# Building the owner matrix of overflow rows: a comparison, a product with ones and a second comparison in place of a comparison and a multiplication

## The reference, cut to what matters

```python
# layer 0
h = jnp.maximum(_layernorm(x, axis=-1), 0.0)
mask = (adj > 0.0).astype(x.dtype)
xj_proj = x @ W1a                                  # here x is h, 64 -> 192
diff = x[:, :, None, :] - x[:, None, :, :]
h = jax.nn.relu(xj_proj[:, :, None, :] + diff @ W1b + b1)
hm = jnp.einsum('bjkh,bjk->bjh', h, mask)          # sum over the neighbours k of node j
deg = jnp.sum(mask, axis=-1)
x = x + hm @ W2 + deg[..., None] * b2
# layer 1
h = jnp.maximum(_layernorm(x, axis=-1), 0.0)
x = x + einsum('bnf,of->bno', einsum('bnm,bmf->bnf', adj, h), W)
```

## Time and profile before

| | |
|---|---|
| median of 3 runs | 916.15 us (915.91 to 916.58) |
| profiled execution, its own time | 916.14 us |
| its span, first to last instruction | 914.0 us |
| around the span | 2.1 us |
| granted TensorE clock, mean | 0.985 |
| VectorE (DVE) busy | 882.5 us, 97% |
| TensorE (PE) busy | 861.5 us, 94% |
| ScalarE (ACT) busy | 775.9 us, 85% |
| GpSimd (POOL) busy | 693.2 us, 76% |
| DVE's share of the chain that ended last | 79% |

### The profile page before, as it was taken

One profiled execution on the slowest core, in us unless ns is written; L12 is line 12 of the kernel. 1 busy time (PEld: TensorE's weight loads), 2 busy tenths in 40 slices (PEclk: granted clock), 3 DMA queues, 4 the chain that ended last, 5 costly groups with the idle time before them and its releaser, 6 DMA issues.

```text
span 914.0 us, 28230 instructions
## 1 busy us (share of the span) xinstructions
PE 861.5 (94%) x8626; PEld 772.5 (85%) x8627; DVE 882.5 (97%) x3544; ACT 775.9 (85%) x1728; POOL 693.2 (76%) x1548
## 2 busy tenths in 40 slices
PE   3869999999999999999999999999999999999996
PEld 1448898889888989898889888888988898889895
DVE  6989999999999999999999999999999999999993
ACT  4858889888888888888888888988888888888883
POOL 0857787878787878787877878787878787878774
PEclk9799999999999999999999999999999999999997
DMA  8500000000000000000000000000000000000000
GB/s 338 240 1 2 8 3 8 8 7 9 8 7 8 2 8 8 8 7 8 7 3 8 8 8 8 8 8 7 3 8 7 8 8 8 8 8 2 7 8 16
DMA packets 8120, 19.21 MB, mean 21 GB/s; under 512 B 1312, under 2 KB 5920, under 8 KB 6944
## 3 DMA queue, kind: packets, MB, share of 16 engines
q1 hardware_dynamic: 7056, 16.98, 4.9%
q10 hardware_dynamic: 912, 0.39, 0.2%
HBM read 13.17 MB, written 4.19 MB: 19 GB/s over the span
## 4 chain that ended last, share of the span: by engine, by line
DVE 79%; issue 15%; POOL 2%; PE 2%; DMA 1%; ACT 1%; SPq 0%; ACTq 0%; POOLq 0%
DVE acc L740 43%; DVE onehot_space L726 16%; DVE onehot_row L783 4%; DVE owner L777 3%; DVE stats L801 3%; DVE PQ L657 3%; DVE x_all L792 2%; DVE mv L769 2%; DVE x_all L795 2%; POOL rstd L894 1%; DMA x_all<-x_nbf_dram 1%; PE ring L336 1%; PE ring L327 0%; ACT mask_all L501 0%; ACT code_jk L503 0%
## 5 line engine op out<-in xcount | busy, mean ns | idle before, releaser
L740 DVE SCALAR_TENSOR_TENSOR acc<-ring,acc 128x384 f32<-128x384 f32 x896 | 488.3, 545 | 4.8
L507 ACT COPY ring<-P 128x768 f32<-128x768 f32 x512 | 403.4, 811 | 25.2 <-DVE acc L740 20.5
L357 PE MATMUL ring<-PQ,onehot_space 128*128 128x192 f16 x4096 | 402.3, 246 | 22.0 <-ACT ring L507 19.1
L357 PEld LDWEIGHTS ring<-PQ,onehot_space 128*128 128x128 f16 x4096 | 338.0, 99 | 43.7 <-DVE onehot_space L726 27.6
L843 POOL TENSOR_TENSOR relu_row<-relu_row 128x192 f32<-128x192 f32 x256 | 154.8, 605 | 117.5 <-ACT relu_row L539 107.4
L726 DVE TENSOR_SCALAR onehot_space<-mask_all 128x256 f16<-128x256 f16 x1024 | 226.6, 237 | 0.0
L560 ACT ACTIVATE h<-x_all,shift,rstd 128x64 f32<-128x64 f32 x128 | 56.2, 439 | 87.1 <-POOL shift L862 87.1
L830 POOL TENSOR_SCALAR start<-P,spare 128x192 f32<-128x192 f32 x128 | 120.4, 941 | 6.1 <-ACT P L553 5.0
L443 PE MATMUL post<-consts,acc 128*128 128x128 f32 x512 | 98.5, 274 | 1.5 <-POOL relu_row L843 1.5
L444 PE MATMUL post<-ownerT,relu_row 128*128 128x128 f32 x512 | 99.0, 275 | 0.0
L385 PE MATMUL ring<-PQ,owner 128*128 128x384 f16 (+1 forms) x512 | 94.5, 307 | 0.0
(11 more groups left out here) (129 smaller groups left out, 1590.1 us busy)
## 6 DMA issues: line engine op xcount, KB each, us to landing
adj_all<-adj_kbj_dram SPq DMA_DIRECT2D x8, 1024.0 KB, 17.9
x_all<-x_nbf_dram SPq DMA_DIRECT2D x8, 512.0 KB, 18.5
out_dram<-x_all SPq DMA_DIRECT2D x32, 128.0 KB, 1.7
consts<-consts_dram SPq DMA_DIRECT2D x1, 192.0 KB, 2.6
onehot_space<-w1a_dram ACTq DMA_DIRECT2D x2, 48.0 KB, 4.4
onehot_space<-w1b_dram ACTq DMA_DIRECT2D x2, 48.0 KB, 6.7
onehot_space<-b_dram ACTq DMA_DIRECT2D x1, 96.0 KB, 10.0
w2a<-w_dram ACTq DMA_DIRECT2D x1, 32.0 KB, 11.1
```

What stands on the lines that cost most here:

```text
L357: last = nc.tensor.matmul(to, hot(s), parts[:, part, H:2 * H], start=False, stop=(part == 1), skip_group_check=True)
L507: return nc.scalar.copy(slots[to], src.unsqueeze(1).unsqueeze(1).broadcast_to([N, BANKS, PER_BANK, H]))
L740: return nc.vector.scalar_tensor_tensor(sums, slots[to][:, bank_], 0.0, start[:, :, :] if first else sums, ALU.max, ALU.subtract if first ...
```

## The change

The owner matrix gets another formula. `reached` is one at (j, r) if r is below `end_row[j]`. `end_row` grows with j, so the number of ones in a column r is the number of nodes whose rows end after r; a product of a 128x128 matrix of ones with `reached` gives this number on every partition. If node j owns r, the nodes j to 127 are those, and their number is `left[j]` = 128 - j, a constant per partition. So `owner` is the comparison of these numbers with `left`. `from_first` and the two instructions L774 and L777 go.

In their place VectorE runs, in step b at i = 2 and behind the three L783, one comparison for `owner` of graph b+1 and one for `reached` of graph b+2. TensorE multiplies the ones with `reached` in step b at i = 0, ahead of the transpose L402, into 128 columns of the bank `post` beside the row codes. ScalarE's copy L544 takes 256 columns in place of 128. Graph 0 gets its product and copy by themselves ahead of the loop, and `left` is summed once while the inputs load.

```diff
-        from_first = sb("from_first", [N, N], F16)
+        reached = sb("reached", [N, N], F16)
+        left = sb("left", [N, 1])
...
-        code_row = sb("code_row", [N, N], F16)
+        row_codes = sb("row_codes", [N, 2, N], F16)
+        code_row, owner_code = row_codes[:, 0, :], row_codes[:, 1, :]
...
 # TensorE, step, i == 0
+                        if exists(b + 1):
+                            pe.wait_ge(reached_ready, b + 2)
+                            nc.tensor.matmul(owner_code_ps, ones_h[:, :], reached[:, :], start=True, stop=True)
                         nc.tensor.matmul(ownerT_ps, own, ident_h[:, :], start=True, stop=True).then_inc(rows_summed, 1)
...
 # TensorE, ahead of graphs
+            pe.wait_ge(reached_ready, 1)
+            nc.tensor.matmul(owner_code_ps, ones_h[:, :], reached[:, :], start=True, stop=True).then_inc(first_summed, 1)
...
 # ScalarE, step, i == 1
-                        nc.scalar.copy(code_row[:, :], code_row_ps)
+                        parts = slice(0, 2 if exists(b + 1) else 1)
+                        nc.scalar.copy(row_codes[:, parts, :], row_codes_ps[:, parts, :])
...
 # ScalarE, ahead of graphs
+            act.wait_ge(first_summed, 1)
+            nc.scalar.copy(owner_code, owner_code_ps).then_inc(first_owner_ready, 1)
...
 # VectorE
-            nc.vector.tensor_tensor(upto, before, ident, ALU.add)
+            chain(nc.vector.tensor_tensor(upto, before, ident, ALU.add))
+            nc.vector.tensor_reduce(left[:, :], upto, AX_X, ALU.add).then_inc(left_ready, 1)
...
+            def owners(b, u):
+                nc.vector.tensor_scalar(owner[:, u % 2, :], owner_code, left[:, 0:1], None, ALU.is_equal).then_inc(owner_ready, 1)
+            def reach(b):
+                nc.vector.tensor_scalar(reached[:, :], count_h[:, :], end_row[:, bass.ds(b, 1)], None, ALU.is_lt).then_inc(reached_ready, 1)
...
-                    if i == 0 and exists(b + 1):
-
-                        if main:
-                            dve.wait_ge(owner_ready, b + 1)
-                        nc.vector.tensor_scalar(from_first[:, :], count_h[:, :], first_row[:, at], None, ALU.is_ge).then_inc(from_ready, 1)
-                    if i == 1 and exists(b + 1):
-                        dve.wait_ge(from_ready, b + 2)
-                        nc.vector.scalar_tensor_tensor(owner[:, (u + 1) % 2, :], count_h[:, :], end_row[:, at], from_first[:, :], ALU.is_lt,
-                                                       ALU.mult).then_inc(owner_ready, 1)
                     if i == 2 and main:
...
                         last.then_inc(onehot_row_ready, 1)
+                        if exists(b + 1):
+                            owners(b + 1, u + 1)
+                        if exists(b + 2):
+                            reach(b + 2)
...
+            reach(0)
             lead(step)
+            dve.wait_ge(left_ready, 1)
+            dve.wait_ge(first_owner_ready, 1)
+            owners(0, 0)
+            reach(1)
             graphs(nc.vector, step, load_any(nc.vector))
```

More of the change, by code:

```diff
@@ L168, in gnn_kernel @@
         h1T_ps = post[:, 3 * N:4 * N]
-        code_row_ps, ownerT_ps = post[:, 0:N], post[:, N:2 * N]
+        row_codes_ps, ownerT_ps = post[:, 0:2 * N].rearrange("p (k n) -> p k n", k=2), post[:, 2 * N:3 * N]
+        code_row_ps, owner_code_ps = row_codes_ps[:, 0, :], row_codes_ps[:, 1, :]
         consts_in = sem("consts_in")
@@ L207, in gnn_kernel @@
         onehot_ready = sem("onehot_ready")
-        from_ready = sem("from_ready")
+        left_ready = sem("left_ready")
+        reached_ready = sem("reached_ready")
+        first_summed = sem("first_summed")
+        first_owner_ready = sem("first_owner_ready")
         owner_ready = sem("owner_ready")
@@ L744, in step @@
                 main = exists(b)
-                at = bass.ds(b + 1, 1)
                 for i in range(CHUNKS):
@@ L782, in step @@
                         for s in range(ROW_SLOTS):
-                            last = nc.vector.tensor_scalar(onehot_row[:, s, :], code_row[:, :], 2.0 * (COVERED + s) + 1.0, None,
+                            last = nc.vector.tensor_scalar(onehot_row[:, s, :], code_row, 2.0 * (COVERED + s) + 1.0, None,
                                                            ALU.is_equal)
                         last.then_inc(onehot_row_ready, 1)
+                        if exists(b + 1):
+                            owners(b + 1, u + 1)
+                        if exists(b + 2):
+                            reach(b + 2)
                     if i == 3 and exists(b - 2):
```

## The result

The changed kernel takes 920.94 us (median of 5 runs, 920.63 to 921.50) against 916.05 (915.81 to 916.58): 1.0053 of the time before, 95% interval 1.0039 to 1.0068. It is slower by 4.9 us.

The account below looks back on a forecast made before the run. VectorE was taken to set the pace, held in places by GpSimd. Per graph +0.19 (leaving L830 later), -0.19 (L830 earlier) and -0.01 gave -1.3 us: 916.14 to 914.8, taken as 915; own range 911 to 921, with rivals 897 to 929.

Parts of the forecast that it names:

- L830 holds the group, and VectorE leaves it at a fixed distance behind L830's start, whatever was saved before: Chunk 2: GpSimd's L830 holds VectorE's three L783 in its first 0.29 or so; they end 0.66 behind its start.
- L830 comes 0.19 earlier: GpSimd's chain: shorter L859, L843 and L862 bring L830 earlier by 0.15 in long graphs, 0.23 in short, 0.19 mean.
- Rival 3: GpSimd's L859 keeps its 700 ns, L830 stays, VectorE leaves later: 936, half the shift 926; chance 0.22 with its halves.
- `owners` and `reach` cost 0.135 each: VectorE, chunk 2: each new comparison costs what an unheld L774 does, 0.135, with bounds 0.10 and 0.33.
- VectorE goes on to L657 0.93 behind L830 in place of 0.74, 0.19 later: VectorE after chunk 2's group: 0.66 for the held three plus 0.27 for the new two, slower by 0.19 a graph.
- +0.19 - 0.19 - 0.01: Sum per graph: VectorE leaves L830 later, L830 comes earlier, an L726 in chunk 3 no longer meets GpSimd; -1.3 us in all.
- The next L726 is held in L774's stead in long graphs: VectorE behind the aggregate: L726 0.23 behind L843 lasts 0.41, so the long graph gains 0.14 there, not 0.33.
- TensorE and ScalarE hide their parts: TensorE's extra matmul, 0.06, fits a 0.19 gap; ScalarE's wider copy, 0.13, is hidden by its wait for L862.
- the forecast's sign: ScalarE's wait for GpSimd's L862 falls by about 0.13, and by as much again as L859 gets shorter.
- TensorE's gathers: What would make the forecast wrong at the root: VectorE waiting for gathers, with about 0.4 less lead over chunk 2's consumes.
- Rivals 1 and 2: First: VectorE not held, GpSimd's L830 gives way, 901, chance 0.2. Second: nothing held, ScalarE and GpSimd limit, 895.5, chance 0.13.
- The plain sum of VectorE's time: VectorE: 0.50 removed, two comparisons added, nothing held differently: 0.22 less a graph, 28 us for 127 graphs.

Follow-up runs that it names:

- the run with constants: Changed kernel with a constant in place of the value per partition in both new comparisons, so the owner matrix is not right: 909.01 us, ratio 0.9922.
- the old places: New formula with `reached` behind the aggregate of chunk 0 and `owner` behind the consumes of chunk 1: 903.44 us, ratio 0.9862 to the kernel before.

## Why the prediction was wrong, step by step

The forecast was 915, hardly a change, with faster (0.47) more likely than slower (0.33). Measured was 920.9, 4.9 slower and clear of no change. The mechanism was found and one term was mis-sized. That 920.9 lies at the edge of the forecast's own 911 to 921 is luck: 921 stood for L830 coming only 0.14 earlier, and it came 0.20 earlier. (The range's other end, a shift of 0.23, gives 910 by the forecast's own sum, not 911.)

- *L830 holds the group, and VectorE leaves it at a fixed distance behind L830's start, whatever was saved before.* Right: in the steady graphs L852 starts about 0.22 ahead of the group, and both the run with the group in chunk 1 and the one with the subtraction first move the time as this says.
- *L830 comes 0.19 earlier.* Right: 4.29 behind L809 in both kinds, 0.16 and 0.24 earlier, 0.20 in the mean; the power L859 fell to 572 ns. Rival 3, which decides below 0.19, is out.
- *`owners` and `reach` cost 0.135 each.* Wrong, this is the step that failed. They cost 0.163 each, 0.056 more in a graph, 7 us. The price was taken from L774 behind the aggregate. The trace of before had it elsewhere too, at 55.11 and 60.21, where its distance to the next start is 0.16:

```profile
60.21 0.24 DVE L774 TENSOR_SCALAR from_first<-count_h,first_row 128x128 f16<-128x128 f16 x1
60.37 0.22 DVE L726 TENSOR_SCALAR onehot_space<-mask_all 128x256 f16<-128x256 f16 x1
```

- *VectorE goes on to L657 0.93 behind L830 in place of 0.74, 0.19 later.* Both are ends, 0.08 longer than the starts; in starts the forecast is 0.85 in place of 0.66. Measured is 0.92 in place of 0.66, 0.26 later. Of the 0.07 too few, 0.056 are the price above, the rest is the three one-hot comparisons (0.59 behind L852's start, not 0.58).
- The sum with what was measured is +0.26 - 0.20 - 0.03 = +0.03 a graph, 4 us; the forecast had +0.19 - 0.19 - 0.01. The -0.03 is the L726 of chunk 3 that no longer meets GpSimd: 0.18 in long graphs before (412.10 to 412.28), 0.13 now. That accounts for the 4.4 us of the graphs.
- *The next L726 is held in L774's stead in long graphs.* Right, but it lasts 0.33 (at 410.75) and not 0.41. It starts 0.34 behind L865 and not 0.23, since the two L741 ahead of the statistics now take 0.39 (409.10 to 409.49) in place of 0.29 before (406.38 to 406.67). The forecast missed that, and a hold of 0.07 on the L741 of chunk 1 (at the second L865). The first is taken up by the hold behind it at L865, as the run with constants shows; for the second the hold by L852 should do the same, but no run takes it away by itself.
- *TensorE and ScalarE hide their parts.* Right, shown by the run with them alone. The copy grew by 0.106, forecast 0.13. ScalarE's wait for GpSimd's L862 fell by 0.28 a graph (87.1 to 51.2 us), as the forecast's sign had it. VectorE does wait for TensorE's gathers, but for 1.7 us in all, in four places (0.2 before).
- Rivals 1 and 2 are out: something is held in every steady graph.

The plain sum of VectorE's time, 28 us less, would have been far off; the old places give 12.5 us.

## What to carry to other kernels

Where VectorE sets the pace and GpSimd runs beside it, an instruction's place relative to GpSimd's is part of its price: the same two comparisons made the kernel 12.5 us faster or 5 us slower. Lay the start times of both engines over one period before moving anything, and price an instruction by the distance to the next start in more than one neighbourhood. A saving ahead of a hold is worth nothing; one behind it counts until the next hold.

## What the runs showed of the hardware

- GpSimd's L852 (one input of 192 columns, 0.94 long in the profile) held a fast 16-bit VectorE instruction until 0.28 to 0.29 after its own start (406.60 here, 404.56 with the subtraction first). The subtraction L891 (two inputs, 0.55) held one until 0.36 (`reached` issued twice) or 0.42 (the subtraction first) after its start, and the first L865 (two inputs, 0.59) until between 0.40 (`reached` ahead of the aggregate) and 0.49 (410.41 here). The Trainium skill (SBUF — State Buffer, "Who interferes with whom") says that of GpSimd and a VectorE instruction in a two-port mode, the one that comes second is blocked for the whole instruction of the other; none of the three agrees.
- The two sides pay differently: started together with the subtraction, VectorE lost 0.36 in one place (401.54), GpSimd 0.08 in another (414.04); over GpSimd's power, GpSimd lost 0.2 and VectorE nothing.
- A value per partition in a comparison of 128 f16 columns costs 0.16 against 0.10 with a constant.
